# A gated cross-attention block on one core: one list of work per engine and step, the last output blocks summed in four banks, the first norm on VectorE

## What is computed

```python
# x: (4,512,512), ctx: (4,512,512)
x = x + tanh(g_xattn) * einsum('emk,enk->emn', q8(layernorm(x)), q8w(ctx))
#   q8: to fp8 and back, one scale for each row and block of 128; q8w: one scale for each 128x128 block
h = layernorm(x) @ (Wa * col_scale)          # 512 -> 1536: q, k (16 heads of 32) and v
a = softmax(causal(q_heads @ k_heads.T / sqrt(32)))
x = x + tanh(g_ffn) * ((a @ v_heads) @ Wp)
```

## Time and profile before

| | |
|---|---|
| median of 3 runs | 514.0 us (513.59 to 514.74) |
| the profiled execution | 513.52 us, its span 511.5 us |
| PE busy | 443.2 us, 87% |
| PE weight loads | 319.0 us, 62% |
| DVE busy | 331.8 us, 65% |
| ACT busy | 273.6 us, 53% |
| POOL busy | 145.2 us, 28% |
| mean granted PE clock | 0.990 |
| chain that ended last | PE 57%, DVE 15%, ACT 12%, SP's queue 6%, DMA 4% |

### The profile page before, as it was taken

The page is one execution under the profiler, slowest core; times in us unless marked ns, Lnnn a source line. Parts: engine busy times, 40 slices in busy tenths (PEclk is TensorE's granted clock), DMA queues, the critical chain, the costliest instruction groups (busy, mean ns, idle before and its releaser), DMA issues.

```text
span 511.5 us, 7890 instructions
## 1 busy us (share of the span) xinstructions
PE 443.2 (87%) x2536; PEld 319.0 (62%) x2536; DVE 331.8 (65%) x1110; ACT 273.6 (53%) x530; POOL 145.2 (28%) x264
## 2 busy tenths in 40 slices
PE   0366886999878999999888999999788999999995
PEld 0244665776544788776555788776455788666763
DVE  4789624588997243688998243678995255565535
ACT  2886226687446542687455552588556333454430
POOL 5667435233214300233214400233222101121110
PEclk9999998999999999999989999999999999999999
DMA  6402154414420244314420244414310243332102
GB/s 227 184 1 84 42 186 97 104 37 99 104 78 1 63 104 140 119 36 100 102 86 3 53 97 120 143 38 99 89 27 2 69 101 88 93 96 72 55 9 82
DMA packets 28024, 42.61 MB, mean 83 GB/s; under 512 B 8272, under 2 KB 8528, under 8 KB 27984
## 3 DMA queue, kind: packets, MB, share of 16 engines
q1 hardware_dynamic: 26448, 41.97, 29.4%
q10 hardware_dynamic: 1536, 0.14, 0.2%
HBM read 12.59 MB, written 4.19 MB: 33 GB/s over the span
## 4 chain that ended last, share of the span: by engine, by line
PE 57%; DVE 15%; ACT 12%; SPq 6%; DMA 4%; issue 2%; POOL 2%; ACTq 1%; POOLq 0%; DVEq 0%
PE pv_bank L731 8%; PE mm_bank L579 7%; PE mm_bank L581 7%; PE mm_bank L580 7%; PE exp_bank L717 5%; SPq L387 5%; DVE x_all L1205 5%; PE max_bank L700 4%; DVE max_bank L1234 4%; ACT work L1005 3%; PE mm_bank L758 2%; PE mm_bank L759 2%; PE mm_bank L760 2%; PE turn_bank L595 2%; DMA col_root<-in_L_ffn_w_rec 2%
## 5 line engine op out<-in xcount | busy, mean ns | idle before, releaser
L1234 DVE CUSTOM_DVE_ANT_0 max_bank<-max_bank,causal 128x512 f32<-128x512 f32 (+3 forms) x256 | 118.9, 516 | 46.9 <-PE max_bank L700 46.9
L495 POOL TENSOR_SCALAR_AFFINE_SELECT work<-work 128x384 f32<-128x384 f32 x64 | 33.5, 524 | 285.4 <-ACT work L1005 285.4
L1005 ACT ACTIVATE work<-exp_bank 128x512 f32<-128x512 f32 (+1 forms) x192 | 91.5, 525 | 39.9 <-PE exp_bank L717 39.5
L731 PE MATMUL pv_bank<-work,v_aug 128*33 128x256 f32 (+3 forms) x512 | 75.2, 436 | 0.0
L700 PE MATMUL max_bank<-k_stack,q_stack 96*128 96x512 f32 (+3 forms) x256 | 61.7, 336 | 12.0 <-DVE row_max L1234 6.0
L717 PE MATMUL exp_bank<-q_stack,k_stack 97*128 97x512 f32 (+3 forms) x256 | 66.5, 351 | 3.6 <-DMA q_stack<-neg_max 1.9
L1217 DVE SCALAR_TENSOR_TENSOR qk_lo<-mm_bank,col_root,qk_hi 128x512 fp32r<-128x512 f32 x32 | 24.0, 749 | 61.3 <-ACT qk_hi L978 61.2
L1205 DVE SCALAR_TENSOR_TENSOR x_all<-mm_bank,coef,x_all 128x128 f32<-128x128 f32 x224 | 60.4, 340 | 2.5 <-PE mm_bank L627 2.5
L700 PEld LDWEIGHTS max_bank<-k_stack,q_stack 96*128 96x128 f32 x256 | 45.3, 192 | 22.7 <-DVE row_max L1234 10.1
L731 PEld LDWEIGHTS pv_bank<-work,v_aug 128*33 128x33 f32 x512 | 27.4, 110 | 47.2 <-issue 40.4
L717 PEld LDWEIGHTS exp_bank<-q_stack,k_stack 97*128 97x128 f32 x256 | 43.7, 191 | 16.2 <-ACT work L1005 4.3
(11 more groups left out here) (161 smaller groups left out, 794.1 us busy)
## 6 DMA issues: line engine op xcount, KB each, us to landing
q_stack<-qk_hi SPq DMA_DIRECT2D x128, 64.0 KB, 2.0
k_stack<-qk_hi SPq DMA_DIRECT2D x128, 64.0 KB, 2.0
x_all<-in_x SPq DMA_DIRECT2D x16, 256.0 KB, 4.1
ctx_raw<-in_ctx SPq DMA_DIRECT2D x16, 256.0 KB, 3.8
q_stack<-qk_lo SPq DMA_DIRECT2D x64, 64.0 KB, 2.0
k_stack<-qk_lo SPq DMA_DIRECT2D x64, 64.0 KB, 2.0
out<-x_all SPq DMA_DIRECT2D x16, 256.0 KB, 2.2
work<-in_L_ffn_Wa SPq DMA_DIRECT2D x3, 768.0 KB, 9.4
```

The costliest lines, as they stand in the source:

```text
L495: pool.affine_select(out=three, in_=three, compare_op=ALU.is_ge, fill=0.0, base=0, pattern=[[0, 3], [1, P]], channel_multiplier=-1)
L731: last = pe.matmul(pv_bank[64 * j:64 * j + D + 1, P * m:T], v_aug[:, m, 2 * u + j, :], prob[j][:, PROB_COL[m]:PROB_COL[m] + T - P * m], st ...
L1005: act.activation(prob[j][:, UNIT_COL[k]:UNIT_COL[k] + UNIT_LEN[k]], exp_bank[(3 * j + k) % 2][:, 0:UNIT_LEN[k]], ACT.Exp, scale=SCALE).the ...
L1234: last = dve.tensor_tensor_reduce(max_bank[unit % 2][:, col:col + width], max_bank[unit % 2][:, col:col + width], causal[:, T - width:T], ...
```

## The change

1. **One sequence for each engine and step.** PE_STEPS, ACT_STEPS, DVE_STEPS, POOL_STEPS and the `_LAST` tables now name every piece of a step, those of the frame too (`max0`..`max5`, `exp0`..`exp5`, `rowmax`, `neg`, `pv`, `copy`, `back`, `norm`, `zero`), so each can stand anywhere. The opening's and the ends' lists are reordered as well.
2. **The first layer norm of x** is one DVE instruction, (x + shift) * rstd, in all batches; the ACT pair is gone.
3. **The last batch's output blocks 2 and 3** are accumulated in PSUM in four banks (the two `max_bank` and the two `mm_bank`) and added to x together: 8 adds instead of 12.
4. **The opening's DMAs.** The k rows of units 0 and 1 are issued by ACT (`D`, head 0) and POOL (`D`, head 1, own semaphores) instead of SP; `w_rec` is loaded first and has a semaphore of its own, for which DVE's `w0` waits instead of for all nine small loads; the opening's inverse deviations of the second norm are made one tile at a time.
5. ACT's first exponential of a step also waits for the weighted values of the step before.

```diff
-PE_GAPS = [
-    ["W0 v3.012", "Q2.0 v3.3", "Q2.1 W1", ""],
-    ["Q2.23 K2.01 W2", "W3", "K2.23", "Q3.0"],
...
-    ["S1", "S2 S3 X1", "S4 S5 X2 S6 S7", ""],
-    ["S8", "", "X3 S9 S10", ""],
-    ["S11 S12", "", "S13 S14 H0", ""],
-    ["S15 H1 A0", "", "H2", ""],
-    ["A1 H3", "q0 k0", "q1.01", ""],
+PE_STEPS = [
+    "max0 max1 rowmax W0 Q2.0 max2 v3.012 exp0 max3 exp1 W1 exp2 Q2.1 exp3 max4 v3.3 exp4 max5 exp5",
+    "Q2.2 max0 max1 rowmax Q2.3 pv exp0 exp1 max2 max3 W2 K2.0 max4 exp2 K2.1 exp3 back K2.2 max5 exp4 exp5 W3",
+    "max0 K2.3 max1 rowmax Q3.0 pv exp0 Q3.1 max2 Q3.2 exp1 max3 max4 back exp2 Q3.3 K3.0 exp3 K3.1 exp4 K3.23 exp5 max5 X0",
+    "max0 rowmax max1 S0 S1 pv max2 S2 max3 X1 max4 exp0 S3 back S4 exp1 exp2 S5 S6 max5 X2 exp3 exp4 exp5",
+    "rowmax max0 max1 S7 pv max2 max3 S8 S9 exp0 max4 exp1 back exp2 exp3 exp4 max5 X3 exp5 S10",
+    "S11 max0 rowmax max1 pv S12 max2 S13 max3 H0 S14 exp0 exp1 max4 exp2 H1 exp3 exp4 S15 exp5 max5 back",
+    "max0 rowmax max1 A0 pv exp0 H2 max2 exp1 exp2 max3 max4 exp3 exp4 max5 exp5 back",
+    "A1 rowmax H3 pv q0.0 exp0 exp1 q0.12 back exp2 q0.3 k0.0 exp3 k0.123 exp4 q1.012 exp5 q1.3 k1.012",
 ]
...
+ACT_STEPS = [
+    "neg W0 exp0 exp1 exp2 W1 exp3 exp4 exp5 v3",
+    "neg Q2 exp0 exp1 copy exp2 W2 exp3 exp4 exp5",
+    "K2 neg W3 copy exp0 C0 exp1 Q3 exp2 exp3 exp4 K3 exp5 X0",
+    "neg C1 copy X1 C2 exp0 exp1 exp2 exp3 exp4 exp5",
+    "neg X2 copy C3 exp0 exp1 exp2 exp3 exp4 exp5",
+    "X3 neg N0 N1 H0 exp0 copy exp1 exp2 H1 exp3 exp4 exp5",
+    "neg N2 N3 exp0 H2 exp1 exp2 copy exp3 exp4 exp5",
+    "H3 neg exp0 copy exp1 c0 exp2 q0 exp3 k0 exp4 exp5 c1",
 ]
...
-DVE_GAPS = [
-    ["", "", "", "x0", "x1"],
-    ["x2 x3 Q2", "", "", "", "m0 m1 m2 e0 m3 K2"],
-    ["", "", "Q3 e1", "", "K3"],
-    ["", "S0 S1", "S2 S3 S4 S5", "", "S6 b0"],
-    ["S7", "S8 b1", "", "", ""],
-    ["S9 S10 S11 t0 t1 S12", "t2 b2", "", "", ""],
-    ["t3 S13 H0 S14 S15 b3 A0", "H1", "", "", "H2"],
-    ["", "A1", "H3 q0", "k0", "q1 k1"],
+DVE_STEPS = [
+    "max0 max1 max2 max3 x0 x1 max4 max5 x2",
+    "x3 max0 max1 L0 Q2 max2 max3 m0 max4 L1 norm max5 L2",
+    "m1 L3 max0 e0 K2 max1 max2 m2 m3 e1 norm max3 max4 Q3 max5",
+    "K3 max0 max1 S0 S1 max2 max3 S2 S3 S4 norm max4 max5",
+    "b0 S5 max0 S6 S7 max1 b1 max2 S8 max3 max4 S9 norm max5",
+    "S10 max0 max1 S11 t0 S12 max2 max3 H0 S13 max4 S14 b2 S15 t1 t2 max5 t3 norm b3 H1",
+    "A0 max0 max1 max2 max3 max4 max5 H2 norm",
+    "H3 A1 norm q0 k0 q1",
 ]
...
 PE_LAST = [
...
+    "Y0 max0 max1 rowmax Y1 pv exp0 max2 exp1 max3 z0 Y2 exp2 exp3 back exp4 max4 exp5 max5 Y3",
+    "max0 rowmax max1 pv max2 exp0 exp1 max3 max4 back exp2 exp3 max5 z1 exp4 exp5",
+    "Y4 rowmax max0 max1 pv max2 max3 exp0 exp1 Y5 exp2 max4 back max5 exp3 exp4 Y6 exp5 Z0",
+    "rowmax z2 pv exp0 exp1 Y7 exp2 exp3 back exp4 exp5",
 ]
...
-PE_FIRST = ("f0 f1 f2 f3 f4 S0 S1 S2 S3 f5 S4 S5 S6 f6 S7 S8 S9 S10 f7 S11 f8 S12 S13 f9 "
-    "S14 S15 v0 v1 f10 f11 q0 B0 k0 V2 B1 q1 M0 k1 M1 M2")
...
+PE_FIRST = ("f0 f1 f2 f3 f4 S0 S1 S2 S3 f5 S4 S5 S6 f6 S7 S8 f7 S9 f8 S10 S11 S12 S13 S14 "
+     "S15 f9 f10 v0 f11 v1 q0 B0 B1 k0 V2 q1 M0 k1 M1 M2")
+
+ACT_FIRST = ("a0 C0 C1 C2 f0 d0 f1 C3 f2 C4 b0 f3 f4 C5 C6 f5 a1 C7 f6 b1 f7 N0 f8 a2 "
+     "a3 N1 f9 N2 b2 f10 N3 b3 v0 f11 v1 q0 k0 c0 V2 D0 c1 p0 q1 D1 k1 c2 c3")
+
+DVE_FIRST = ("x0 w0 x1 x2 x3 t0 t1 L0 L1 t2 t3 L2 A0 A1 T0 F0 F1 L3 F2 F3 T1 T2 c0 S0 "
+     "S1 S2 S3 b0 S4 S5 S6 S7 S8 b1 S9 S10 S11 S12 b2 S13 h0 S14 S15 b3 T3 h1 u0 u1 "
+     "h2 u2 h3 u3 B0 q0 B1 k0 M0 q1 M1 M2 k1")
+
+POOL_FIRST = ("i0 s0 s1 s2 s3 s4 s5 o0 s6 j0 s7 r0 j1 l0 l1 r1 l2 l3 r2 r3 j2 j3 g0 g1 "
+     "D0 g2 D1 g3 p0")
...
 END_LAST = {
-    "PE": "P0 Z4 Z5 Z6 Z7 T0 z3 Z8 Z9 Z10 Z11",
-    "ACT": "T0 z3",
-    "DVE": "T0 Z6 z3 Z7 Z8 Z9 Z10 Z11",
+    "PE": "Z1 Z2 pv Z3 back Z4 Z5 z3 Z6 Z7 Z8 Z9 Z10 Z11",
+    "ACT": "copy z3",
+    "DVE": "z2 Z1 Z2 norm Z3 z3 Z8 Z9 Z10 Z11",
 }
...
+        def stack_rows(eng, u, w, j, done=None):
+
+            g, s = u // 2, u % SLOTS
+            dst, parts = ((q_stack, (qk_hi, qk_lo, qk_hi)), (k_stack, (qk_hi, qk_hi, qk_lo)))[w]
+            rows = slice(D * (2 * (u % 2) + j), D * (2 * (u % 2) + j) + D)
+            for a, part in enumerate(parts):
+                eng.dma_start(dst[D * a:D * a + D, s, j, :].bitcast(FP32),
+                              part[rows, g % 2, w, :].bitcast(FP32)).then_inc(done or s_stack[s], 16)
...
+        def last_sum(i):
+
+            return (max_bank[0], max_bank[1], mm_bank[0], mm_bank[1])[i]
...
+                bank = last_sum(i) if g else mm_bank[i % 2]
...
+                    pe.matmul(bank[:], y_h, wp_hi[:, k, :], start=(k in (0, 2)), stop=False)
+                    pe.matmul(bank[:], y_h, wp_lo[:, k, :], start=False, stop=False)
+                    last = pe.matmul(bank[:], y_l, wp_hi[:, k, :], start=False, stop=(k in (1, 3)))
+                if g in PART_ADDS:
+                    last.then_inc(s_part, 1)
...
-                act.activation(buf, x_tile(n, i), ACT.Identity, bias=shift1[:, i:i + 1]).then_inc(s_xc, 1)
-                act.wait_ge(s_xc, NT * n + i + 1)
-                act.activation(buf, buf, ACT.Copy, scale=rstd1[:, i:i + 1]).then_inc(s_xn, 1)
...
+                if j == k == 0 and b + u:
+                    act.wait_ge(s_pv, 8 * b + u)
...
+            def norm(n, i):
+                dve.wait_ge(s_rstd1, n + 1)
+                dve.wait_ge(s_turn, 12 * n + i + 1)
+                dve.tensor_scalar(tile_buf[:, i, :], x_tile(n, i), shift1[:, i:i + 1], rstd1[:, i:i + 1],
+                                  ALU.add, ALU.mult).then_inc(s_xn, 1)
```

320 lines of the change are left out of this document (129 added, 191 removed), and 34 rows, old and new, of tables (ACT_GAPS, ACT_LAST, BEFORE, BEFORE_LAST).

## The result

| | before | after |
|---|---|---|
| median | 513.8 us (4 runs) | 500.3 us (499.74 to 501.92) |
| profiled execution, its span | 513.52, 511.5 | 499.74, 497.9 |
| ratio after to before | | 0.9742 [0.9713, 0.9771] |
| PE busy, DVE busy, ACT busy | 443.2, 331.8, 273.6 | 440.6, 340.3, 255.7 |

What follows compares the result with a forecast made beforehand. PE was taken to bound most of a batch and DVE a window in steps 3 to 6. Opening -4.1, three batches +2.4 and last batch -2.0 sum to -3.7, giving 510.3 us (506.5 to 513; wider range 504.5 to 515.5).

Steps and rivals of the forecast that it cites:

- Part 1, the opening: Start to first row-max transpose: reordered lists and k rows issued by ACT and POOL gain 4.1 us, from -1.0 to -6.2.
- (a): Opening: w0 waits for w_rec alone, so POOL's first scaling starts near 16.5, 0.4 us earlier.
- (c): Opening's order: first product-add near 32.2, last statistics near 52.9 (3.4 us earlier), q0 1.7 us earlier.
- (b): Opening and batches: the norm of x moved from ACT to DVE, 0.57 us each, changes nothing on the path.
- (d): Opening's k rows issued by ACT and POOL: unit 0 ready 1.5 us earlier, unit 1 and the first transpose 4.1 earlier.
- T1: Theory made after the result: the k rows' second wait and its aftermath make most of the opening's 7.3 us.
- rival D: Opening: POOL's k rows land late, at the column loads' 9.45 us; +2.7 us, so 516.7; chance 0.05.
- Part 2, the batches: Three batches: PE-bound steps change by 0; in step 6 DVE waits for PE behind H2's turn; +0.8 each, +2.4 in all.
- rival B: Window: PE's order makes DVE wait in steps 3 and 6, 2.6 us a batch; 515.7; chance 0.13.
- Part 3, the last batch: Last batch: four banks, eight adds and new order gain 2.5 us, step 5 loses 0.5; -2.0, from -0.5 to -3.0.
- A: Reordering gives all: q0 follows the statistics, no wait at H2, tail -2.5; -10.5 us, so 503.5; chance 0.20.
- C: Whole kernel: the window's loss and the rest's gain cancel, 514.0 us; chance 0.10.

Runs made afterwards that it cites:

- e1: Kernel after, with the k rows of units 0 and 1 issued by SP again: 504.9 us, ratio 0.9823.
- e14: Kernel before, with 15 matmuls that nobody reads while PE waits for the second k rows: ratio 0.9979.
- e2: e1 with the opening's four lists of before as well, the first norms kept on DVE: 506.4 us, ratio 0.9852.
- e8: Kernel after, with the batches' norm of x as ACT's two activations again, all orders else new: 502.0 us, ratio 0.9766.
- e16: Kernel after, with 12 matmuls that nobody reads ahead of step 6's row-max transpose in batches with a successor: 497.8 us, ratio 0.9684.
- e17: Kernel after, with the last output summed in two banks and 12 adds, the order else new: 501.9 us, ratio 0.9765.
- e9: Kernel after, with steps 3 to 6 of before and POOL's lists of steps 4 to 7 of before: 500.6 us, ratio 0.9739.
- e3: Kernel after, with the batch steps of before, norms still on DVE at places the author chose: 511.9 us, ratio 0.9960.
- e4: Kernel after, with the last batch's lists of before, two banks and twelve adds: 504.8 us, ratio 0.9821.
- e5: Kernel after, with the three batches as before, norm on ACT; only opening and last batch new: 501.9 us, ratio 0.9764.
- e7: Kernel after, with steps 0 to 2, 7 and the end of before, norm on ACT; steps 3 to 6 new: 502.4 us, ratio 0.9775.
- e15: Kernel after, with the exponentials' scores issued in pairs on PE in all four batches: 511.6 us, ratio 0.9953.
- e6: Kernel after, with steps 3 to 6 of the three batches in the old order, POOL's lists still new: 505.4 us, ratio 0.9833.
- e10 to e13: Kernel after, four reorderings around step 6: H2 later; max5 early; both; A0 ahead with H2 last: 506.5, 505.7, 505.3, 506.9 us.
- e18: e16 with H2's turn behind max3 on PE and N3 last on ACT: 503.6 us, ratio 0.9797.

## Why the prediction was off, step by step

**Part 1, the opening (-4.1 forecast, -7.3 measured).** (a) and (c) were right: POOL's first scaling at 16.08 (16.5), first product-add at 31.68 (32.2), last statistics at 52.41 (52.9). Wrong in (c) was only what follows: I put both value products behind H2's turn at 54.3, but PE had v0 at 51.15 and q0 at 59.70. (b), the norm: 0.56 us each (0.57 taken):
```profile
L1168 DVE TENSOR_SCALAR tile_buf<-x_all,shift,rstd 128x512 f32<-128x512 f32 x12 | 6.7, 560 | 1.3 <-POOL rstd L473 1.2
```
(that is the batches' twelve). In the opening L3 took 1.28 us beside POOL's scaling, against 0.54 alone, so the extra was 0.7 and not 0.4; here the trace agrees with the Trainium skill (SBUF — State Buffer, "Who interferes with whom") in that VectorE and GpSimd can hold each other up. That VectorE stood still for the whole of POOL's 1.04 us the records do not show: L3 ended 0.28 us behind POOL's scaling, half of its own 0.54.

The step that failed is (d), in two terms. First, I let `D1` wait until c1, p0 and q1 ahead of it had run, 79.7: ACT issued it at 73.01, while p0, which stands ahead of it in the list, ran only from 73.28 to 75.18, and q1's high part from 75.08. PE's last product of q1, for which that high part waits, began at 72.58. So an issue there waited for semaphores, its own and those of what stands ahead of it, and not for the activations ahead of it to end. So the rows were there before PE wanted them, and the 3.59 us of the earlier trace rows went whole. Second, I left out the clock: e1 shows that the wait is followed by half clock worth 2.4 us, e14 1.24 us of it in the kernel before. (d) is worth 6.0 of the 7.3 (e1, by the span; 4.2 by the ratios), the lists 1.1 to 1.5 (e2). T1 is shown. POOL's rows took 2.0 to 2.1 us to land, as its lower bound said, so rival D's 9.45 did not occur. DVE ran nothing beside POOL's issues (68.1 to 74.2), so the rule of the Trainium skill on blocked descriptors (SBUF — State Buffer, "SBUF: two separate sides") was not put to the test.

**Part 2, the batches (+2.4 forecast, -2.2 measured).** The failed step is "PE carries the same matmuls and was already without idle time, so 0": the three windows took 3.9 us more (+0.9, +1.0 and +2.0), so the PE-bound parts took 6.1 less. 12.75 busy of 12.80 is no proof, since lengths of the same shape fell at an unchanged clock, and between step 7 and the window there was visible idle time too (1.1 of 74.4 us). In one period 1.3 to 1.5 us of waits went and 0.5 to 0.7 of matmuls moved into the window, 1.8 in all from transpose to transpose and 2.2 from ACT's mark to mark. The last sentence of the prediction named exactly this case. The norm, put at nothing, costs about 1 us a batch if it goes back to ACT in the new order (e8), as ACT's exponentials are on PE's path in step 1. In the window the term was about right in size (+1.0 in batch 1, 42.75 instead of the kernel before's 41.76; forecast +1.4). My working had a slip: 40.6 and the waits of 0.9 and 0.7 give 42.2, not 42.6. At full clock (e16) the window takes 42.10 and 42.12 us in batches 0 and 1 and DVE waits 0.95 and 0.54, which is the mechanism as forecast; what I had not foreseen is the clock, which adds 0 to 0.6 in the kernel after, 1.4 in e17, and hides H2's wait. With the window's order of before (e9) the time was the same, so the term bought or cost nothing that shows. C2 ahead of exp0 in step 3 cost nothing, as said (11.0 us from mark to mark instead of 11.7); rival B fell with it. By step after:
```profile
88.50:99.10 10.60, 10.60 (x78) 7.86 (x77) 9.44 (x31) 5.43 (x12) 3.94 (x9) 1.00 0.39 93
110.40:121.40 11.00, 9.40 (x72) 6.08 (x70) 10.85 (x43) 7.69 (x17) 4.78 (x8) 1.00 0.38 92
121.40:131.20 9.80, 9.27 (x56) 5.87 (x56) 9.73 (x40) 6.73 (x15) 1.53 (x4) 1.00 0.42 101
```
Beside the earlier trace rows, step 1 went from 12.8 to 10.6 us with 78 matmul records instead of 89, step 3 is still DVE-bound at 10.85 of 11.00. Part of step 1's difference is work that the new lists put elsewhere; only whole periods compare.

**Part 3, the last batch (-2.0 forecast, -4.0 measured).** The end was nearly right: 24.24 us from step 7's transpose (23.8 forecast, 24.95 before with Y7 outside), the four banks 2.1 us (e17). To the last add it took 20.6 (21.2 forecast, 22.4 before), and the store behind it 3.7 instead of 2.5 (2.6 forecast). On one chip the store took 3.5 with the new end (e1, e2, e3) and 2.6 with the old (e4), on another 2.6 with the new (e5, e7, e8), so whether the new end lengthens it is open. The failed step is "step 5 costs 0.5": steps 0 to 6 gained 3.3, of which 1.15 are moved matmuls (Y7 among them) and 2.2 PE's waits, 0.6 of them visible before (64.21 busy of 64.78) and the rest in records, the exponentials' above all (477 to 432 ns and 356 to 306): the same blind spot as in part 2. That order alone made it, e17 shows; which of its moves did stays open, since the pairs of exponentials account for 0.6 us (e15).

**The rivals.** A (503.5) came nearest, and one of its reasons was right, q0 earlier; that there would be no wait at H2 was not. B, C and D fell. What none had was PE's waits in the batches and the clock behind a wait.

**Open.** The parts undone one at a time (e2 5.7, e4 4.1, e5 1.1 by the ratios) sum to 10.9 of 13.3 us; by spans without the store they sum to more than the whole. Whether that is the spread between chips and executions was not shown. Of the other orders of the window one (e9) was the same and the rest (e6, e10 to e13, e18) 3 to 6 us slower; whether a better one exists is not settled.

## What to carry to other kernels
Don't read a bound from PE's busy share alone: compare the mean of one shape's records between places of the same granted clock, and suspect a wait in the excess over the shortest. Price a wait of PE with the slow clock that may follow it, not only by its own length, and expect that part to differ between executions; where the wait can't be removed, matmuls that nobody reads cover it (1 to 3 us of 500 here). And before moving a piece, follow its chain to the next step, since in a dense order the wait moves to the chain's other end.

## What the runs showed of the hardware
- Behind 3.1 and 4.1 us in which PE stood still (step 6 of the kernel after, the opening of e1) the granted clock of the windows was 0.50 to 0.76, where full speed is 1.00 (2.4 GHz) and 0.50 is 1.2 GHz. The weighted values (16 matmuls) took 3.98 to 4.48 us instead of 2.35, and step 0 lost 1.2 to 2.4 us. Twelve matmuls that nobody reads brought 2.35 back in the gap of step 6, and the kernel to 497.8 us. The clock did not fall alike behind alike gaps: behind 3.1 us the values took from 3.30 us (0.70) to 4.48 (0.50), behind 1.9 us from 2.35 (1.00, e7 and e8) to 4.04 (0.58, e17).
- ACT issued a DMA at 73.01 although two activations that stand ahead of it in the list ran from 73.28 to 75.18 and from 75.08. POOL's issues took 0.50 to 0.77 us each, and its 64 KB rows landed in 2.0 to 2.1 us (medians from issue to landing), ACT's in 2.3 to 2.5.
- A 128x512 fp32 instruction of DVE over SBUF took 0.54 us alone and 1.28 beside a scaling of POOL, whose own length stayed at 1.04.
